# Two expert passes made one loop: results added into the output in DRAM, each token's second row copied ahead, deeper buffers, expert numbers loaded pair by pair

## The reference, cut to what matters

```python
xn = _layernorm(x, axis=-1)                       # x: (6250, 256)
x = x + _L0_gnn_ref(xn, ...) + _L0_mix_ref(xn[None], ...)[0]
x = x + _L0_ffn_ref(_layernorm(x, axis=-1)[None], ...)[0]

def _L0_ffn_ref(features, ...):
    rh = jax.nn.relu(features @ router_w1 + router_b1)
    expert_logits = jax.nn.softmax(rh @ router_w2 + router_b2, axis=-1)
    top_w, top_i = jax.lax.top_k(expert_logits, 2)          # 2 of 6 experts
    routing_weights = jax.nn.softmax(top_w, axis=-1)
    h1 = relu(einsum('bsd,edh->bseh', features, expert_w1) + expert_b1)
    h2 = relu(einsum('bseh,ehf->bsef', h1, expert_w2) + expert_b2)
    expert_out = einsum('bsef,efo->bseo', h2, expert_w3) + expert_b3
    return sum over the two chosen experts of routing_weight * expert_out
```

## Time and profile before

| | |
|---|---|
| Median of three runs | 787.16 us |
| The profiled execution | 785.95 us, of which its span is 783.9 us |
| PE busy | 677.8 us (86%) |
| PE weight loads busy | 621.5 us (79%) |
| DVE busy | 556.7 us (71%) |
| ACT busy | 440.9 us (56%) |
| POOL busy | 403.3 us (51%) |
| DMA | 106.24 MB, mean 136 GB/s |
| Chain that ended last | PE 74%, DVE 10%, DMA 4%, ACT 3%, issue 3%, POOL 2% |
| Mean granted TensorE clock | 0.938 of full speed |

### The profile page before, as it was taken

One profiled execution on the slowest core, in us unless ns is written; L12 is line 12 of the kernel. 1 busy time (PEld: TensorE's weight loads), 2 busy tenths in 40 slices (PEclk: granted clock), 3 DMA queues, 4 the chain that ended last, 5 costly groups with the idle time before them and its releaser, 6 DMA issues.

```text
span 783.9 us, 15402 instructions
## 1 busy us (share of the span) xinstructions
PE 677.8 (86%) x4705; PEld 621.5 (79%) x4705; DVE 556.7 (71%) x1423; ACT 440.9 (56%) x878; POOL 403.3 (51%) x446
## 2 busy tenths in 40 slices
PE   3877999999999888888860899999994799999992
PEld 2867788888888777777750799999993799999992
DVE  5674679888888867777864377777773477777772
ACT  2645566667777446767740465565651565656551
POOL 3465378876666100464444155556554155565553
PEclk9999999999999999989855699999998899999997
DMA  8885644544443454765144524444433534544420
GB/s 220 194 163 125 152 128 132 143 132 119 122 138 107 139 164 156 246 192 180 53 112 118 165 82 139 142 133 135 141 111 103 154 93 130 149 133 147 134 65 29
DMA packets 72463, 106.24 MB, mean 136 GB/s; under 512 B 24612, under 2 KB 45605, under 8 KB 72386
## 3 DMA queue, kind: packets, MB, share of 16 engines
q1 hardware_dynamic: 51074, 72.57, 32.9%
q0 software_dynamic: 21312, 32.69, 13.7%
HBM read 60.32 MB, written 46.78 MB: 137 GB/s over the span
## 4 chain that ended last, share of the span: by engine, by line
PE 74%; DVE 10%; DMA 4%; ACT 3%; issue 3%; POOL 2%; SPq 1%; POOLq 0%; DVEq 0%; ACTq 0%
PE kv_ps L1348 11%; PE kv_ps L1350 10%; PE kv_ps L1349 10%; PE pt L1340 6%; PE d_ps L1212 5%; PE kv_ps L1189 5%; PE kv_ps L1192 4%; PE kv_ps L1190 4%; PE xt_ps L1340 3%; PE kv_ps L1289 2%; PE pt L1189 2%; PE pt L1192 2%; PE pt L1190 2%; POOL tab L571 1%; PE pt L1280 1%
## 5 line engine op out<-in xcount | busy, mean ns | idle before, releaser
L1348 PE MATMUL kv_ps<-we_h,now_h 128*128 x648 | 194.2, 300 | 11.0 <-DVE now_l L1159 4.8
L1350 PE MATMUL kv_ps<-we_h,now_l 128*128 x648 | 185.2, 286 | 0.0
L1349 PE MATMUL kv_ps<-we_l,now_h 128*128 x648 | 185.1, 286 | 0.0
L1348 PEld LDWEIGHTS kv_ps<-we_h,now_h 128*128 128x128 f32 x648 | 125.7, 194 | 15.7 <-issue 15.7
L1349 PEld LDWEIGHTS kv_ps<-we_l,now_h 128*128 128x128 f32 x648 | 125.8, 194 | 0.0
L1350 PEld LDWEIGHTS kv_ps<-we_h,now_l 128*128 128x128 f32 x648 | 125.5, 194 | 0.0
L1137 DVE TENSOR_TENSOR work<-kv_ps,be 128x256 f32<-128x256 f32 x216 | 81.7, 420 | 61.0 <-PE kv_ps L1350 60.7
L582 POOL TENSOR_TENSOR arena<-work,arena 128x256 f32<-128x256 f32 x80 | 53.3, 686 | 105.2 <-ACT work L768 105.2
L775 ACT ACTIVATE now_h<-pt 128x512 fp32r<-128x512 f32 x54 | 32.2, 597 | 112.3 <-PE pt L1340 112.3
L539 POOL DMA_INDIRECT alg<-al_tab,src_all x50 | 62.2, 1244 | 40.1 <-issue 25.9
L947 DVE TENSOR_REDUCE ss<-xring 125x16 f32<-125x1040 f32 x50 | 61.7, 1234 | 17.3 <-ACT xring L653 16.3
(11 more groups left out here) (239 smaller groups left out, 1833.5 us busy)
## 6 DMA issues: line engine op xcount, KB each, us to landing
arena<-tab SPq DMA_DIRECT2D x40, 259.0 KB, 3.0
xring<-in_x SPq DMA_DIRECT2D x26, 224.0 KB
xt_tab<-arena SPq DMA_DIRECT2D x10, 568.8 KB
arena<-tab SPq DMA_DIRECT2D x40, 131.0 KB, 2.1
we_h<-wt_h SPq DMA_DIRECT2D x6, 768.0 KB, 5.5
we_l<-wt_l SPq DMA_DIRECT2D x6, 768.0 KB, 7.7
weight_in<-tab SPq DMA_DIRECT2D x14, 259.0 KB, 3.0
xring<-in_x SPq DMA_DIRECT2D x5, 560.0 KB
```

The lines of the kernel that those rows point to most:

```text
L1348: pe.matmul(outp, hi[:, c, :], we_h[:, w], start=c == 0, stop=False)
L1349: pe.matmul(outp, hi[:, c, :], we_l[:, w], start=False, stop=False)
L1350: last = pe.matmul(outp, lo[:, c, :], we_h[:, w], start=False, stop=c == KC - 1)
```

## The change

- **One loop.** The two passes become one loop over `ALL = 54` pairs (`tiles`, `has`), in which pair 27 follows pair 26 as any pair follows another.
- **Output by adding.** In the mix stage SP stores each step's x2 rows straight to the output (`out_t`), 25 stores of two tiles. The experts' weighted results are then added to the output in DRAM by accumulating scatters (`add_rows`, `compute_op=ALU.add`), in both passes. POOL waits for all additions of pass 0 before the first one of pass 1, since both touch the same tokens.
- **Second rows ahead.** The row for the second choice no longer carries a sum. It is copied from `rb` to `tab1` as it was loaded, by a plain scatter of 262 numbers (`second_rows`): pairs 0 to 7 before the loop, then pair n + 8 (`AHEAD = 8`) after the additions of pair n.
- **Buffers.** 14 row buffers of 262 numbers replace 7 of 518, in the same memory. Results go to a ring `yw` of 7 buffers; ACT writes the scaled third bias there itself, so POOL's addition (L582) is gone. SP loads pair n when the additions and the copies of pair n - 14 have landed.
- **Expert numbers** are loaded for each pair (two numbers, `EL = 1`) into one of four register sets.

The core of the diff:

```diff
-U = 7
-U1 = 5
-EL = 3
+U = 14
+U1 = 10
+EL, SETS = 1, 4
+ALL = 2 * PAIRS
+AHEAD = 8
+YB = 7
+CB = 6
...
+                g = group_of(i)
+                at = 2 * i - tiles_of(g)[0]
+                sp.wait_ge(x2_done, i + 1)
+                wide(out_t[:, 2 * i:2 * i + 2, :], xr[g % RB][:, at:at + 2, 0:D], x2_out[g % RB])
...
-            for k in range(2):
-                if k == 1:
-                    sp.wait_ge(tab_done, 2)
-                    for u in range(U):
-                        sp.wait_ge(z_out[u], 16 * HB * uses(u, PAIRS))
-                    sp.wait_ge(fill_out[1], 16 * (E + 1))
-                for j in range(PAIRS):
-                    load(k, j)
+            for n in range(ALL):
+                k, j = n // PAIRS, n % PAIRS
+                for h in range(HB):
...
+                    if h == 0 and n >= U:
+                        sp.wait_ge(*added(n - U))
+                        if n - U < PAIRS:
+                            sp.wait_ge(*copied(n - U))
+                    if n == PAIRS and h == 0:
+                        sp.wait_ge(fill_out[1], 16 * (E + 1))
+                        for m in range(PAIRS - CB, PAIRS):
+                            sp.wait_ge(*copied(m))
+                    sp.dma_start(rb[n % U][:, h, :], (tab0, tab1)[k][bass.ds(first, S), :]).then_inc(r_in[n % U], 16)
...
-                        pool.tensor_tensor(row[:, 0:D], b3w[n % 2][:, h, :], row[:, D:2 * D] if k == 0 else row[:, 0:D],
-                                           ALU.add).then_inc(b3w_done, 1)
...
+            def second_rows(n):
+                u = n % U
+                pool.wait_ge(r_in[u], 16 * HB * (turn(n) + 1))
+                if n >= CB:
+                    pool.wait_ge(*copied(n - CB))
+                for h in range(HB):
+                    pool.indirect_dma_start(
+                        out=tab1, out_offset=bass.IndirectOffsetOnAxis(
+                            ap=rb[u][:, h, C_POS:C_POS + 1].bitcast(I32), axis=0),
+                        in_=rb[u][:, h, :], in_offset=None, bounds_check=E * REG - 1, oob_is_err=False
+                    ).then_inc(second_out[n % CB], 16)
+            def add_rows(n):
+                u = n % U
+                for h in range(HB):
+                    pool.wait_ge(y_done, n * HB + h + 1)
+                    pool.indirect_dma_start(
+                        out=out, out_offset=bass.IndirectOffsetOnAxis(
+                            ap=rb[u][:, h, C_TOK:C_TOK + 1].bitcast(I32), axis=0),
+                        in_=yw[n % YB][:, h, :], in_offset=None, bounds_check=N - 1, oob_is_err=False, compute_op=ALU.add
+                    ).then_inc(z_out[n % YB], 16)
+            for n in range(AHEAD):
+                second_rows(n)
+            for g in range(GROUPS - RB, GROUPS):
+                pool.wait_ge(x2_out[g % RB], stored(g))
+            for n in range(ALL):
+                if n == PAIRS:
+                    for m in range(PAIRS - YB, PAIRS):
+                        pool.wait_ge(*added(m))
+                add_rows(n)
+                if n + AHEAD < PAIRS:
+                    second_rows(n + AHEAD)
...
-                    for h in range(HB):
-                        w = D + C_W + k
-                        act.activation(b3w[n % 2][:, h, :], b3_sb[:, bass.ds(es[j, h] * D, D)], ACT.Copy,
-                                       scale=rb[n % U][:, h, w:w + 1]).then_inc(b3w_ready, 1)
+                if n >= YB:
+                    act.wait_ge(*added(n - YB))
+                for h in range(HB):
+                    w = C_W + n // PAIRS
+                    act.activation(yw[n % YB][:, h, :], b3_sb[:, bass.ds(es[n, h] * D, D)], ACT.Copy,
+                                   scale=rb[n % U][:, h, w:w + 1]).then_inc(b3w_ready, 1)
```

More of the change, by code:

```diff
@@ L208, in gps_layer @@
         fill = sb("fill", [1, 2, EP], I32)
-        rb = [(arena, weight_in)[u >= U1][:, at:at + HB * ROW1].rearrange("p (b n) -> p b n", b=HB)
-              for u in range(U) for at in (u % U1 * HB * ROW1,)]
+        rb = [rows[:, u * HB * ROW:(u + 1) * HB * ROW].rearrange("p (b n) -> p b n", b=HB)
+              for rows, count in ((arena, U1), (weight_in, U - U1)) for u in range(count)]
         WT = HB * KC * S
@@ L223, in gps_layer @@
         hs1, hs2 = rows_of(work, 0), rows_of(work, HB * F)
-        b3w = [rows_of(work, HB * F * (2 + b)) for b in range(2)]
+        yw = [rows_of(rows, at) for rows, at in [(work, HB * F * (2 + b)) for b in range(4)] + [(xring, E * D), (xring, E * D + HB * F), (staged, 2 * HB * D)]][:YB]
         b3_sb = xring[:, 0:E * D]
@@ L318, in scattered, with stored, experts @@
             return 16 * sum(2 * SIZES[a] for a in range(g % RB, g + 1, RB))
-        def experts(engine, regs, k, j):
-            part = regs[(j // EL) % 2]
+        def stored(g):
+            return 32 * sum(SIZES[a] for a in range(g % RB, g + 1, RB))
+        def experts(engine, regs, n):
+            k, j = n // PAIRS, n % PAIRS
+            part = regs[(n // EL) % SETS]
+            if j == 0:
+                engine.wait_ge(e_done, k + 1)
             engine.load(part, tab_e[0:1, k, j * HB:(j + EL) * HB])
@@ L326, in expert_regs, with tiles, has, added @@
         def expert_regs(engine, name):
-            return [[engine.alloc_register(f"{name}{h}_{i}") for i in range(EL * HB)] for h in range(2)]
-        def tiles(engine, k, regs, step):
+            return [[engine.alloc_register(f"{name}{h}_{i}") for i in range(EL * HB)] for h in range(SETS)]
+        def tiles(engine, regs, step):
             es = {}
[L333 to L337, removed]
+            for n in range(-1, ALL + 2):
+                if has(n) and n % EL == 0:
+                    for i, e in enumerate(experts(engine, regs, n)):
+                        es[n + i // HB, i % HB] = e
+                step(n, es)
         def turn(n):
             return n // U
[L342 to L346, removed]
+        def has(n):
+            return 0 <= n < ALL
+        def added(n):
+            return z_out[n % YB], 16 * HB * (n // YB + 1)
+        def copied(n):
+            return second_out[n % CB], 16 * HB * (n // CB + 1)
         block = ctx.enter_context(nc.Block())
@@ new lines, in normal, with third_bias @@
+            def normal(n):
+                act.wait_ge(r_in[n % U], 16 * HB * (turn(n) + 1))
+                for h in range(HB):
+                    row = rb[n % U][:, h, :]
+                    act.activation(xe[:, n % 2, h, :], row[:, 0:D], ACT.Identity,
+                                   bias=row[:, C_NMR:C_NMR + 1], scale=row[:, C_R:C_R + 1]).then_inc(xe_done, 1)
+            def third_bias(n, es):
+                if n >= YB:
[4 more added lines that the diff above has]
+                                   scale=rb[n % U][:, h, w:w + 1]).then_inc(b3w_ready, 1)
@@ L791, in _ @@
+            normal(0)
+            tiles(act, act_e, step)
         @block.vector
@@ new lines, in plus_bias, with weighted @@
+            def plus_bias(rows, outp, layer, n, es, finished):
+                for h in range(HB):
+                    dve.tensor_tensor(rows[:, h, :], outp[:, h, :], be[layer][:, bass.ds(es[n, h] * F, F)], ALU.add).then_inc(finished, 1)
+            def weighted(n):
+                dve.wait_ge(l3_done, n + 1)
+                dve.wait_ge(b3w_ready, (n + 1) * HB)
+                for h in range(HB):
+                    w = C_W + n // PAIRS
+                    dve.scalar_tensor_tensor(yw[n % YB][:, h, :], l3_ps[n % 2][:, h, :], rb[n % U][:, h, w:w + 1], yw[n % YB][:, h, :],
+                                             ALU.mult, ALU.add).then_inc(y_done, 1)
@@ L1390 @@
+            tiles(pe, pe_e, step)
 def kernel(**inputs):
```

228 lines of the change are left out of this document (82 added, 146 removed).

## The result

The changed kernel took 757.17 us (median of four runs, 755.42 to 757.82), the kernel before beside it 786.73 us: a ratio of 0.9626, with a 95% interval of 0.9605 to 0.9646. The forecast was 762.2 us, so the gain was 29.6 us where 25.0 were foreseen. Runs are therefore compared within their job, and the gap is the subject of its own part.

The account below looks back on a forecast made before the run. PE's own work was taken to bound the experts within a pass, with idle and slow time between passes. Gains of 19.75 (border) and 5.21 (register loads), together 24.96 us, took 787.16 to 762.2 us; range 757 to 779.

Parts of the forecast that it names:

- The border: Between the passes, pairs 24 to 29: removing the drain, hole, refill and slow clock was to gain 19.75 us.
- if pair 27's rows are there in time: Condition on the gain between the passes: first rows of pass 1 ready at 570.3 us, needed by PE at 585.4.
- The slack at the border: Between pair 27's rows being normalized and PE turning them, 15.1 us were to be left.
- The sum's own formula: POOL up to pair 18 falls behind by 19 x (2c - 3.06) us, at c us per addition.
- the second rival: Accumulating scatters issue slower, so copies are late between the passes: 765 to 786 us, chance 0.08.
- one of the prediction's own signs of being wrong: In the changed profile, ACT waiting for a DMA at the third bias or at normalizing would show the forecast wrong.
- The rule on descriptors: For POOL's accumulating scatters, two read descriptors per chunk would raise issue from 1.28 to about 1.8 us, still hidden.
- The argument against it: Against slower accumulating scatters on POOL: plain ones issue in 977 to 1027 ns whatever goes on beside them.
- The register loads: In the experts' beats, two-number loads were to cost PE nothing, gaining 5.21 us.
- The waits named as hidden: POOL's wait for all additions of pass 0 was to hide in one beat: 5.62 us against 2.56 issuing, 3.0 landing.
- The mix stage: The 25 added stores, 6.4 MB between 305 and 397 us, were to cost nothing; upper bound 26 us.
- the one that reached 786: The rival of slower accumulating scatters: at double price, 2.56 us, 24 us lost between the passes; its range's chance 0.08.

Follow-up runs that it names:

- control of job 3: The changed kernel unaltered, timed again beside e10 and e11: 756.63 us, ratio 0.9643 to the kernel before; the same run as e9.
- e11: The changed kernel with each copy issued behind one addition, in place of two additions and then two copies: 757.68 us, ratio 0.9658.
- e12: The changed kernel with each copy issued behind one addition and copies six pairs ahead in place of eight: 770.09 us, ratio 0.9791.
- e3: The changed kernel with plain scatters to the output in place of accumulating ones, so the last writer of a row stays: 819.59 us, ratio 1.0419.
- e2: The changed kernel with six expert numbers loaded at each third step into two register sets again: 787.75 us, ratio 1.0016.
- e6: The changed kernel without the 25 stores of x2 rows in the mix stage and their waits: 781.2 us, ratio 0.9932.
- e9: The changed kernel unaltered, timed in a later job: 756.63 us, ratio 0.9643 to the kernel before.
- e5: The changed kernel unaltered, timed in a later job: 780.77 us, ratio 0.9914 to the kernel before.
- e10: The changed kernel without POOL's 54 copies, pass 1 loading the rows of pass 0 once more: 758.66 us, ratio 0.9667.
- e1: The kernel before, with two expert numbers a load in four register sets as the one edit: 784.49 us, ratio 0.997.
- job 1: The series of timings on one chip that holds e1, e2 and e3, without the unaltered changed kernel; one of those with long beats.

## Why the prediction was right, and where it was not

- **The border.** 19.75 us foreseen, 19.79 measured. The mechanism was right: SP no longer waits for finished rows, and PE works through. That its condition held, "if pair 27's rows are there in time", was luck, as the next point shows.
- **The slack at the border.** Wrong, and the step that failed first is the price of an accumulating scatter: 1.28 us start to start was taken, 1.86 measured. The sum's own formula gives 15.1 - 19 x (2 x 1.86 - 3.06) = 2.6 us with it, and with POOL's measured 6.42 us a pair 15.1 - 19 x (6.42 - 5.62) = -0.1. The point at which the second rival would have begun to decide, 1.93 us, was 0.07 us away. The trace gives the slack term by term. The copies of pair 26 end at 574.67 us in place of 562.1, 12.6 later (15.5 by POOL's pace, less 2.9 for additions that begin at 452.92 in place of 455.8). SP's load begins 1.4 us behind them in place of 5.0, but takes 4.3 us in place of 2.1. And ScalarE needs the rows 4.4 us sooner than was taken (579.87 in place of 585.4 - 1.1 = 584.3): it works in the order of its program, and there normalizing stands well ahead of PE's turn. 12.6 - 3.6 + 2.1 + 4.4 = 15.5 us, against 15.1 of slack: ScalarE was 0.4 us late. In the control of job 3 it was 2.6 us late and 1.5 us of a beat were lost, in e11 1.2 us late and 0.2 lost, and in e12 copies 12.4 us later cost 13.8 us more. ScalarE waiting for a DMA at normalizing was one of the prediction's own signs of being wrong. The forecast held by less than a microsecond and not by the 15.1 that it claimed.
- **The rule on descriptors.** The Trainium skill ("Collectives: The Full Stack", section "The bandwidth ceiling: the fold count and why AG ≠ RS ≠ AR") gives two read descriptors to an adding chunk, from which the prediction estimated about 1.8 us. Half more on all of the 1.28 us, as it says, would be 1.92; about 1.8 comes out if only the 0.98 grows and the 0.30 of pause stays. The trace agrees with the size: 1.86. It can't show read descriptors by themselves, but an addition has 144 packets where a plain scatter has 48. The argument against it, that plain scatters never issue above 1.03 us, was no argument on an adding one, and e3 shows that it is the adding which takes 1.55 in place of 0.98.
- **The register loads.** 5.21 us foreseen, 5.51 measured. Two numbers take 0.54 us on TensorE and make no beat longer; e2 shows the stall of every second load of six. The beat is 5.613 us now, which is 0.3 of it.
- **POOL and the DMA.** The waits named as hidden are: POOL's for the additions of pass 0 took 2.4 us, and nobody waited for it. Additions land in 3.9 us, not 3.0, also hidden. POOL's queue was to come to 43% if an addition took three times a copy; from 440 to 580 us it is at 43.0%.
- **The mix stage.** Nothing foreseen; e6 shows nothing beyond the 0.3 us above.
- **Start and end.** Nothing foreseen, 1.29 and 2.61 us gained. These 3.9 us are most of the 4.6 by which the gain was larger than forecast. Of the start, 0.9 us is there at the last table scatter (422.51 and 423.39 us); in e9 that scatter ends where it did before the change, and pair 0 is turned 1.4 us earlier than in the first profile all the same. So it moves by as much as the gain from run to run. The end repeats: from pair 51 it is 22.6 us in e5 and e9 as well. Without adding it is 1.2 us longer (e3), without copies 2.1 us (e10), so both seem to have a part in it; why is open.
- **What was not foreseen at all** is the other time, 781 us. None of the rivals had it, not even the one that reached 786, since it worked through the border, and the long beats are spread over pass 0. By the forecast's own range (757 to 779) that job lies outside, so it was luck too which kind of job gave the first result.

Still open: what differs between the jobs. It isn't the kernel, nor the chip by itself, and the kernel before, whose POOL issues two scatters in a row in this stage (four at the end of each pass), doesn't feel it (784.9 to 786.9 us in all five jobs). e1, which has that same POOL program and ran in job 1, shows it in a trace: within its passes no wait for a layer's product is over 0.7 us, and its beats are 5.62 us. That a burst of POOL's issues holds the updates is read from timelines; the changed kernel without copies in such a job, which would prove it, was not had. e3 doesn't fit simply either: its POOL has less to do (5.1 us a pair), its holds are longer (up to 6.1 us in pass 0, with four beats of 13 us), and even in pass 1, with two scatters in a row, five waits are 1.0 to 1.5 us and some beats 5.9 to 6.0.

## What to carry to other kernels

An operation that no row shows should be priced by what it must do more than its relative that is shown, and the plan laid out so that the higher price still fits: here the higher price used up all of a slack of 15 us. Slack is to be counted to the instruction that takes the data in its engine's own order (ScalarE's normalizing), not to the one behind it that the sum is about (PE's turn). Work that is moved ahead of a border is only as early as the engine that issues it, so count that engine's whole period, and not the time from the last item. And a kernel that keeps POOL issuing without a pause should be timed in several jobs before its gain is believed.

## What the runs showed of the hardware

- An accumulating indirect scatter of 128 rows of 1 KB is 1.55 us long and starts 1.86 us after the one before it; the plain one 0.98 and 1.28. It lands 3.9 us (median) after its start, the plain one to the same tensor 2.7 us in the kernel before. It has 144 packets, the plain one 48.
- In two jobs of five (the one of the first result counted), VectorE and ScalarE waited for TensorE's results up to 3.9 us in e5, and VectorE up to 6.1 us in e3, while POOL issued indirect DMAs one behind the other. With two in a row and a pause no wait was over 0.7 us in e5 and e1, but five were 1.0 to 1.5 us in e3.
- A load of two numbers into registers takes 0.49 to 0.54 us on ScalarE, VectorE and TensorE (medians); loads of six stalled TensorE at every second one, by 0.57 us a beat (e2).
- TensorE, idle for the most part from about 583 to 595 us in e12, had its clock granted at the lower level from 586.5 to 600.2 us, the first 5 us of work behind the hole included.
- The program ends 5.2 us after POOL's last accumulating scatter in the changed kernel and 7.1 us in e10; after the last plain one 9.1 us in the kernel before and 7.7 us in e3. No run here says why.
